# Attention weights' second pass: rows turned one step ahead by transposition, own rows' product first

## The reference, cut to what matters

```python
def _L2_gnn_ref(h, src, dst, W, b):
    ...
    alpha = e_exp / e_sum[dst]
    out = jax.ops.segment_sum(h[src] * alpha, dst, num_segments=n)
    return out
x = _layernorm(x + _L2_gnn_ref(x, src, dst, L2_gnn_W, L2_gnn_b), axis=-1)
```

## Time and profile before

| | us |
|---|---|
| median of three runs (3369.0, 3370.6, 3388.2) | 3370.6 |
| the profiled execution | 3348.0 |
| its span, first to last instruction | 3346.2 |
| second pass, first `scale` to the end of the last `D3` | 1775.86 to 1956.98 |

### The profile page before, as it was taken

The page is one execution under the profiler, slowest core; times in us unless marked ns, Lnnn a source line. Parts: engine busy times, 40 slices in busy tenths (PEclk is TensorE's granted clock), DMA queues, the critical chain, the costliest instruction groups (busy, mean ns, idle before and its releaser), DMA issues. The chain is left out here.

```text
span 3346.2 us, 53978 instructions
## 1 busy us (share of the span) xinstructions
PE 2459.9 (74%) x14171; PEld 1675.7 (50%) x14171; DVE 2486.4 (74%) x4558; ACT 1724.2 (52%) x3950; POOL 1925.5 (58%) x1870
## 2 busy tenths in 40 slices
PE   3976666666578789979946779998999998995000
PEld 1543444444467667745525556665666656663000
DVE  5569999999777758859966747776566665888553
ACT  3784444444222258858841126665566655775221
POOL 4008888887488800068870047775655437886776
PEclk9988787787777888879977989998999998997555
DMA  4133333433466668733313445555445543332111
GB/s 129 64 96 87 107 99 107 109 106 98 119 199 196 191 144 180 153 104 115 112 46 75 113 127 167 157 162 159 135 136 141 139 106 108 112 114 68 47 47 27
DMA packets 742887, 393.28 MB, mean 118 GB/s; under 512 B 517090, under 2 KB 649265, under 8 KB 742770
## 3 DMA queue, kind: packets, MB, share of 16 engines
q1 hardware_dynamic: 691582, 333.94, 36.4%
q0 software_dynamic: 51200, 58.03, 6.8%
HBM read 217.18 MB, written 175.64 MB: 117 GB/s over the span
## 5 line engine op out<-in xcount | busy, mean ns | idle before, releaser
L1341 POOL DMA_INDIRECT g_W<-t,g_cols x400 | 463.2, 1158 | 260.8 <-PE g_pS L2901 116.4
L460 POOL DMA_INDIRECT fr_W<-in_x,fr_idx x400 | 496.0, 1240 | 127.6 <-issue 107.7
L1341 POOL DMA_INDIRECT me_W<-t,me_cols x200 | 236.0, 1180 | 58.0 <-issue 46.9
L1341 POOL DMA_INDIRECT ou_W<-t,ou_cols x200 | 222.6, 1113 | 58.1 <-issue 40.8
L3433 POOL DMA_INDIRECT de_V<-t,de_cols x200 | 215.8, 1079 | 53.6 <-issue 41.4
L3117 POOL DMA_INDIRECT out<-ou_F,ou_ways x200 | 200.1, 1000 | 77.5 <-issue 53.3
L1058 PE MATMUL at_pL<-at_XF,w_logit 128*128 128x512 f32 x100 | 89.7, 996 | 123.0 <-ACT at_XF L1105 123.0
L1331 POOL COPY g_cols<-pos 128x8 int32 (+1 forms) x50 | 19.8, 396 | 241.2 <-POOLq L85 241.0
L1331 POOL COPY de_cols<-pos 128x8 int32 (+1 forms) x25 | 8.1, 324 | 261.4 <-POOLq L85 261.2
L931 ACT ACTIVATE me_nzt<-me_pXT 128x512 f32<-128x512 f32 x47 | 28.1, 598 | 170.9 <-PE me_pXT L914 170.9
L914 PE MATMUL at_pXT<-ident,at_nz 128*128 128x128 f32 x200 | 40.3, 336 | 93.8 <-ACT at_nzt L931 52.3
(11 more groups left out here) (619 smaller groups left out, 8536.8 us busy)
## 6 DMA issues: line engine op xcount, KB each, us to landing
mg_y<-wanted SPq DMA_DIRECT2D x50, 256.0 KB
at_nx<-in_x SPq DMA_DIRECT2D x50, 256.0 KB, 2.6
x<-at_nz SPq DMA_DIRECT2D x50, 256.0 KB, 3.3
x1T<-at_nzt SPq DMA_DIRECT2D x50, 256.0 KB, 2.9
t<-up_X SPq DMA_DIRECT2D x100, 128.0 KB, 2.0
t<-g_HS SPq DMA_DIRECT2D x50, 256.0 KB
t<-g_HD SPq DMA_DIRECT2D x50, 256.0 KB, 3.4
g_D<-t SPq DMA_DIRECT2D x50, 256.0 KB
```

The source lines that it names most:

```text
L460: self.nc.gpsimd.indirect_dma_start(out=self.W[w][b][:, (2 * t + h) * C:(2 * t + h + 1) * C], out_offset=None, in_=self.table, in_offset=b ...
L1341: nc.gpsimd.indirect_dma_start(out=slot(w, b, t), out_offset=None, in_=table, in_offset=bass.IndirectOffsetOnAxis(ap=cols[w][:, c:c + 1], ...
```

## The change

Each half is turned with one product and three transpositions in place of four products. `turn` and `scale` run one step ahead: PE turns half b of step q+1 as soon as the scan of that half of step q has left `pA`. The own rows' product comes first in a step and opens the sum in `pB`. Its signal, `back`, now only says that `D` is free; the new signal `centred` counts the halves of `back`, and ACT and the scans wait for it.

```diff
-                def turn(q, w):
+                def turn(q, w, b):
                     pe.wait_ge(e["scaled"], q + 1)
...
+                        if n == 0:
+                            t.matmul(to, WS[w][:, m:m + C], k.ident[:, :], start=True, stop=True)
+                        else:
+                            i = t.transpose(to, WS[w][:, m:m + C], k.ident[:, :])
+                    i.then_inc(e["turned"], 1)
...
+                def own(q, w):
                     pe.wait_ge(own_in[w], ring_uses(q, w, 16))
...
-                    t.matmul(pB[w][:, :], k.ident[:, :], D[w][:, :], start=False, stop=True, skip_group_check=True)\
+                    t.matmul(pB[w][:, :], k.ident[:, :], D[w][:, :], start=True, stop=False, skip_group_check=True)\
                         .then_inc(e["back"], 1)
 
-                def step(q, r, w):
-                    if q is not None:
-                        turn(q, w)
-                        back(q, w)
+                def back(q, w, b):
+                    pe.wait_ge(e["summed"], last_of(q, b))
...
+                    i.then_inc(e["centred"], 1)
+
+                def step(q, w, more=True):
+                    own(q, w)
+                    for b in range(2):
+                        if more:
+                            turn(q + 1, 1 - w, b)
+                        back(q, w, b)
...
-                    act.wait_ge(e["back"], q + 1)
+                    act.wait_ge(e["centred"], 2 * q + 2)
...
-                    reuse(dve, e["back"], q)
+                    if not isinstance(q, int) or q >= 1:
+                        dve.wait_ge(e["centred"], 2 * q + (b - 1))
...
-                def step(q, r, w):
-                    if q is not None:
-                        scale(q, w)
+                def step(q, r, w, more=True):
+                    if q is not None and more:
+                        scale(q + 1, 1 - w)
```

More of the change, by code:

```diff
@@ L2344, in attention2_stage @@
         e = {n: g.sem(n) for n in ("starts", "steps", "weighed", "pe_mid", "exped", "alpha", "scaled", "turned",
-                                   "summed", "back", "sq", "sumsq", "ln", "dev", "norm", "over")}
+                                   "summed", "centred", "back", "sq", "sumsq", "ln", "dev", "norm", "over")}
         left = lambda ap: ap[:, ::-1]
@@ L2397, in _ @@
                 i.then_inc(e["pe_mid"], 1)
-                def turn(q, w):
+                def turn(q, w, b):
                     pe.wait_ge(e["scaled"], q + 1)
[L2401 to L2410, removed]
+                    if not isinstance(q, int) or q >= 1:
+                        pe.wait_ge(e["summed"], 2 * q + (b - 1))
+                    for n in range(CT):
+                        m = (b * CT + n) * C
+                        to = pA[b][0:C, n * P:n * P + P]
+                        if n == 0:
[4 more added lines that the diff above has]
+                def own(q, w):
                     pe.wait_ge(own_in[w], ring_uses(q, w, 16))
@@ L2414, in back @@
                         pe.wait_ge(e["over"], q - 1)
-                    for b in range(2):
[L2416 to L2420, removed]
-                    t.matmul(pB[w][:, :], k.ident[:, :], D[w][:, :], start=False, stop=True, skip_group_check=True)\
-                        .then_inc(e["back"], 1)
-                def step(q, r, w):
-                    if q is not None:
-                        turn(q, w)
-                        back(q, w)
-                pe.wait_ge(e["alpha"], 2)
-                by_step(pe, step)
+                    t.matmul(pB[w][:, :], k.ident[:, :], D[w][:, :], start=True, stop=False, skip_group_check=True)\
+                        .then_inc(e["back"], 1)
+                def back(q, w, b):
+                    pe.wait_ge(e["summed"], last_of(q, b))
+                    for n in range(CT):
+                        m = (b * CT + n) * C
+                        i = t.matmul(pB[w][:, m:m + C], S[b][:, n * P:n * P + P], k.center[0:C, 0:C],
+                                     start=False, stop=b == 1 and n == CT - 1, skip_group_check=True)
+                    i.then_inc(e["centred"], 1)
+                def step(q, w, more=True):
+                    own(q, w)
+                    for b in range(2):
+                        if more:
+                            turn(q + 1, 1 - w, b)
+                        back(q, w, b)
+                pe.wait_ge(e["alpha"], 2)
+                for b in range(2):
+                    turn(0, 0, b)
+                step(0, 0)
+                step(1, 1)
+                step(2, 0)
+                with pe.Fori(0, ITERS // 2 - 2) as j:
+                    step(2 * j + 3, 1)
+                    step(2 * j + 4, 0)
+                step(ITERS - 2, 1)
+                step(ITERS - 1, 0, more=False)
             @block.scalar
@@ L2573, in step @@
                                         over(k.dinv[:, bass.ds(r * G, G)], C), ALU.mult).then_inc(e["over"], 1)
-                by_step(dve, step)
+                scale(0, 0)
+                step(0, None, 0)
+                step(1, 0, 1)
+                step(2, 1, 0)
+                with dve.Fori(0, ITERS // 2 - 2) as j:
+                    step(2 * j + 3, 2 * j + 2, 1)
+                    step(2 * j + 4, 2 * j + 3, 0)
+                step(ITERS - 2, ITERS - 3, 1)
+                step(ITERS - 1, ITERS - 2, 0, more=False)
+                step(None, ITERS - 1, 1)
 def gcn1_stage(nc, k, out):
```

## The result

The changed kernel takes 3399.05 us (median of 15 runs, 3386.7 to 3412.4) against 3378.3 for the kernel before (15 runs beside them, 3358.6 to 3388.2): ratio 1.0069, interval [1.0049, 1.0089]. It is slower, by 20.8 us where 47 were forecast.

What follows compares the result with a forecast made beforehand. Bounds: the chain from second scan to sum of squares, then PE's clock. With the clock down, 8.5 + 208.2 + 13.3 gives 230 us against 181, +49, taken as +47; 3370.6 + 47 = 3417, range 3400 to 3434.

Steps and rivals of the forecast that it cites:

- Which clock: PE in the second pass: the clock rises at most once near the start, falls within a few steps, stays down; 0.73.
- Rival 1: Second pass: the clock stays up and only the chain counts, -7 to -14 us, 3357 to 3364; chance 0.16.
- The step at 1.2 GHz: Second pass at the low clock: PE sets a period of 9.05 us, with 1.26 per half's turn; pass 230 against 181.
- one more switch: PE's turn of a half at 1.2 GHz: another switch between product and transposition, some 0.1 us per half, giving +54.
- The full-clock step: Second pass at 2.4 GHz: chain 2.73 us instead of 2.97, so 6.58 per step, 0.24 less.
- The median: Baseline: differences summed against the profiled 3348.0 us were added to the median of the runs shown, 3370.6, giving 3417.
- The clock argument: PE in the second pass: the change removes the sixteen-pass run ahead of every rise; thin groups and 1.6 us waits lose the clock.
- The chances: Whole kernel: slower by more than about 1% (34 us) 0.70, same 0.28, faster 0.02.
- rival 2: Second pass: the clock alternates to the end, steps of 6.58 to 9.05 us, mean 7.8, +23, 3394; chance 0.10.

Runs made afterwards that it cites:

- the filled kernel: The changed kernel with six more products of 128 columns, which nothing reads, behind each own product: 3336.7 us, ratio 0.9909.
- Three more looks: The kernel before, unchanged, profiled three more times: executions of 3377.6, 3376.9 and 3381.7 us, second pass 213.0, 203.6 and 210.4 us.
- the exchanged one: The changed kernel with `back` of a half called before the turn of that half of the next step: 3336.2 us, ratio 0.9926.

## Why the prediction was right, and where its size was not

- **Which clock: right.** At most one rise near the start, a fall within a few steps, and 0.50 to the end: one rise, 6.8 us, then 0.50. Filling the wait, with the change otherwise kept, brings the clock and the time back, which shows the cause. What it is in PE's work that keeps the clock stays open: the filling changes the amount of work, the waits and the longest run at once. (Rival 1 speaks of two falls; the prediction works out one, behind 1790.3.)
- **Rival 1: wrong here.** The clock fell at about 1790 us although PE had not idled longer than 1.62 us (the wait at 1788.36; 1.6 were worked out). By the rule of the Trainium skill (TensorE: Matmul & The Clock Gate, Part 1: The HAM clock gate), a fall after an idle stretch, it would have stayed up, as the prediction says.
- **The step at 1.2 GHz: nearly.** 9.25 to 9.33 us for 9.05. A half took 1.40 from its first pass to `back` (1833.56 to 1834.96), where 1.26 was taken from a place in which transpositions followed; twice 0.14 makes 9.33 of 9.05, and the estimate of 0.1 per half for one more switch named it. The pass came to 232.2 against 230 worked out, +51 in the profiles.
- **The full-clock step: right.** 6.58 worked out, 6.57 to 6.65 in the filled kernel.
- **The median: wrong, and this is the step that failed.** "[T]heir spread (3369.0 to 3388.2) lies elsewhere as far as one profile tells. I add the differences to the median": the profile's pass of 181.1 us was not the median's. Three more looks have 203.6 to 213.0, 209.0 on average, and 232.1 - 209.0 = 23 us is the measured 20.8 within the spread of the totals outside the pass (3164.6 to 3173.3 in these looks). The hint stood in the times before: the profiled execution was 21 us below the fastest of the three runs shown. The clock argument should have been turned on the kernel before too: its step was as close to losing the clock as its own first 36 us showed.
- **The chances:** 0.70 stood on slower by over 1%, and 0.69% was measured; the mis-sized baseline alone moved it there. The limit was too coarse as well: I took 1% as what can be told from no change, and the interval is 0.2% to either side.
- **Luck.** 3399.05 lies just below the prediction's own range of 3400 to 3434, but the difference of 20.8 is far below its +38 to +54. The time came that near because the median of before was 3378.3 in the larger set, 7.7 above the 3370.6 that the forecast was added to. It also lies close to rival 2's 3394, and not by rival 2's reason: the clock of the changed kernel did not alternate, that of the kernel before did.

## What to carry to other kernels

Where a stage's clock alternates, count what an edit takes from PE's work before counting what it saves on the chain: shortening and spreading PE's passes can halve its clock, and idle PE time filled with harmless passes can be worth more than the edit. Which property of those passes counts, their number, their length or the waits between them, these runs do not separate. Before a sum is made against one profile, compare that execution with the plain runs; if it lies below all of them, its stage times are not the median's. And what is moved out of the chain must be weighed against what is moved in: with the turn behind `back` instead of ahead of it the same change is a gain (ratio 0.9926), in part by the shorter chain and in part by the higher clock (0.70 for 0.50).

## What the runs showed of the hardware that was not expected

- PE busy nearly all the time did not lift the clock: 199.56 of 214 us busy at 0.50 in the changed kernel, and 10 us without a break at 1.2 GHz in the exchanged one (1853.34 to 1863.47).
- The kernel before has two regimes within one pass: 6.82 us per step at 1.00 once it locks (from 1811 us in the first profile), 6.8 to 9.3 otherwise; three of four executions never locked or locked late.
- Twelve float32 transpositions of 128 columns keep the clock as six two-pass products do (0.97 and 0.96 between 1790 and 1950 us).
